# Starting the aggregation products on Y's upper half before the last five adjacency rows are prepared, and moving part of the column sums to TensorE

## The chip, the cores and the metric

The kernel runs on one core of a Trainium2 chip. The metric is the device time of one execution in microseconds (us); lower is better. A core has TensorE (PE, matrix products and transposes), VectorE (DVE), ScalarE (ACT), GpSimd (POOL) and SyncE (SP), which here issues nearly all DMAs. The engines run their own instruction lists in order and wait for each other on semaphores.

## The reference: what is computed

Inputs are x (8 batches, 2048 nodes, 128 features) and adj (2048 x 2048), all in float32. Cut to what matters:

```python
HW = einsum('bnf,fo->bno', layernorm(x), W)
A  = relu((adj + adj.T) * 0.5)
D  = sum(A, axis=1)
d  = where(D > 0, D ** -0.5, 0)
L  = eye(N) - d[:, None] * A * d[None, :]
x  = x + relu(einsum('nm,bmo->bno', L, HW))
x  = x + moe(layernorm(x))      # tokens + 8 gated experts, top 2, GELU between two 128x128 products
```

The change touches only the part before and around the first rows of the einsum with L.

## The kernel before, in words

**Layout.** The nodes are cut into 16 blocks of 128. S = relu(adj + adj.T) is symmetric, so only its lower triangle of 136 blocks of 128 x 128 is kept (`s_tri`). The features of half of the batches (4) lie side by side as 512 columns: Y, in 16 node blocks, is HW scaled by d. Each float32 operand of the large products is split in a high and a low part (`y0_hi`, `y0_lo`, `stage[..][hi, lo]`), and a block of a product is three 128 x 512 matmuls.

**Stage one, the setup loop.** The rows of S are made from j = 15 down to 0; r = 15 - j counts them. For one row SP loads the row of adj (`low`) and its column (`up`) into one of nine slots; PE transposes the column's blocks into PSUM (`turn`, in groups of four, 40 groups in all), DVE adds the row (`add`), ACT applies relu in place and sums along the row (`relu`). POOL and, for j = 5 to 1, DVE add each row to running column sums (`add_columns`). A node's degree is its row sum plus its column sum; the sum over partitions of column block k is a product with a column of ones (`column_sum(k)`). Between the rows, a job k (0 to 15) brings one node block of x: SP loads it (`load`), DVE takes mean and variance (`statistics`), POOL inverts (`invert`), PE transposes it (`turn_x`) and multiplies by W (`project`), ACT copies (`copy_x`) and keeps the result in `hw0` (`keep`). `JOBS` says how many jobs go ahead of each row: 2 for rows r = 0 to 3, then 1 each for r = 4 to 11.

**Degrees.** `degrees(0)` on DVE finishes blocks 8 to 15, POOL takes the power -1/2 (`root(0)`), ACT makes the high part of Y (`y_high(m)`) and DVE the low part (`y_low(m)`); `degrees(1)` and `root(1)` do blocks 7 to 0.

**Stage two, the products.** Unit u of the einsum is node block 15 - u. Its matrix operand is staged: blocks that lie in the triangle as they are (`high_direct`, `low_direct`), the others transposed by PE in groups of four (`turn_group(u, g)`), copied by ACT (`high_group`) and finished by DVE (`low_group`). Units 0 and 1 are made in four parts of eight blocks each: unit 0 with Y's blocks 15 to 8, unit 1 with the same, unit 0 with blocks 7 to 0, unit 1 with those. From unit 2 on a unit is one run of sixteen blocks, and while it runs the next one's operand is staged. After the 32 units (16 for each half of the batches) come the expert layers.

**Order.** All of it is written out by hand: each engine's function lists its steps, with tables such as `JOBS`, `RELU_AT`, `ADD_AT` and `PARTS_AT` for what stands between the `y_high`/`y_low` steps.

## Time and profile before

| | |
|---|---|
| median of 3 runs | 878.15 us (875.48 to 878.35) |
| the profiled execution | 877.46 us, of which the traced span is 875.7 us |
| TensorE busy | 839.2 us, 96% of the span |
| VectorE, ScalarE, GpSimd busy | 639.1, 476.0 and 324.7 us |
| first product of unit 0, first product of unit 2 | 78.62 us and 108.07 us from the span's start |

Times below are from the start of the span. Names such as L692 are lines of the kernel. In the trace a float32 matmul that isn't a transpose is listed as two matmuls (a 128 x 1 column sum counts x2), a transpose as one. Matmuls are pipelined: a listed duration reaches past the start of the next one, so spacing is read from the start times.

### The profile page before, as it was taken

To read this page: it belongs to the slowest core of one execution; us is meant where nothing else is said; L and a number is where in the kernel's file an instruction comes from. 1 tells how busy PE (TensorE), PEld (TensorE's weight loads), DVE (VectorE), ACT (ScalarE), POOL (GpSimd) and SP (SyncE) were. 2 spreads that over 40 slices of the span, in tenths; PEclk is the share of its full clock that TensorE was granted. 3 is DMA by queue.
4 is the path that set the end of the run, shared out by engine and by line. 5 is a ranking of instruction groups with operands and counts; after the bars stand their busy time and mean duration, and the time that the engine had idled before them with its cause. 6 is when DMAs were issued, how large, how long until landed. Compare 5 with 4: busy or idle time off the path is not lost.

```text
span 875.7 us, 14324 instructions
## 1 busy us (share of the span) xinstructions
PE 839.2 (96%) x4098; PEld 697.3 (80%) x4098; DVE 639.1 (73%) x1553; ACT 476.0 (54%) x871; POOL 324.7 (37%) x318
## 2 busy tenths in 40 slices
PE   3687999999999999999999999999999999999998
PEld 3676788888888888888888777788888888888886
DVE  3678645479889644443515599999999999999997
ACT  2686523224333201021110488888888888888886
POOL 1893163474757545555445539101000000000000
PEclk9999999999999999999999999999999999999999
DMA  9991576686866257977778876778767777778772
GB/s 277 325 311 53 220 284 253 240 277 237 272 221 202 85 181 285 334 273 263 255 280 315 303 249 230 267 281 294 289 272 265 257 274 277 273 290 292 286 266 82
DMA packets 93472, 223.00 MB, mean 255 GB/s; under 512 B 8904, under 2 KB 60128, under 8 KB 81520
## 3 DMA queue, kind: packets, MB, share of 16 engines
q1 hardware_dynamic: 88304, 213.23, 68.7%
q0 software_dynamic: 2608, 8.33, 2.4%
q10 hardware_dynamic: 2512, 0.86, 0.4%
q8 instruction: 24, 0.39, 0.2%
q14 instruction: 24, 0.20, 0.1%
HBM read 157.89 MB, written 64.49 MB: 254 GB/s over the span
## 4 chain that ended last, share of the span: by engine, by line
PE 90%; DVE 4%; ACT 2%; DMA 2%; issue 1%; DVEq 0%; ACTq 0%; SPq 0%
PE bank L989 13%; PE bank L991 13%; PE bank L990 13%; PE bank L1489 6%; PE bank L1473 6%; PE bank L1475 6%; PE bank L1486 6%; PE bank L1474 6%; PE bank L1487 6%; PE bank L344 3%; PE bank L936 2%; PE bank L1495 2%; PE bank L474 1%; PE bank L325 1%; DMA b_sb<-in_L_ffn_b 1%
## 5 line engine op out<-in xcount | busy, mean ns | idle before, releaser
L1531 ACT ACTIVATE act_h<-bank,b_sb 128x512 f32<-128x512 f32 x256 | 176.3, 689 | 46.8 <-PE bank L1475 42.5
L1573 DVE TENSOR_TENSOR gated<-c_all,act_h 128x512 f32<-128x512 f32 x256 | 177.4, 693 | 25.5 <-ACT act_h L1531 20.4
L1578 DVE TENSOR_TENSOR g_lo<-gated,g_hi 128x512 fp32r<-128x512 f32 x256 | 175.1, 684 | 0.2
L1538 ACT ACTIVATE g_hi<-gated 128x512 fp32r<-128x512 f32 x256 | 159.5, 623 | 6.1 <-DVE gated L1573 6.1
L1449 POOL DMA_DIRECT2D out<-fin x31 | 23.6, 762 | 308.6 <-DVE fin L1586 308.6
L1105 POOL TENSOR_SCALAR z<-x,mv,rstd 128x128 f32<-128x128 f32 x128 | 106.9, 848 | 3.4
L989 PE MATMUL bank<-y_hi,stage 128*128 128x512 f32 x256 | 105.4, 412 | 2.8 <-issue 1.6
L1051 ACT ACTIVATE z_hl<-bank 128x512 fp32r<-128x512 f32 x32 | 19.1, 597 | 156.4 <-PE bank L936 156.4
L1473 PE MATMUL bank<-z_e,w_hi 128*128 128x512 f32 x256 | 102.8, 402 | 0.1
L1489 PE MATMUL bank<-g_lo,w_hi 128*128 128x512 f32 x256 | 100.9, 394 | 1.1 <-DVE g_lo L1578 1.1
L989 PE MATMUL bank<-y,stage 128*128 128x512 f32 x256 | 101.2, 395 | 0.0
L1486 PE MATMUL bank<-g_hi,w_lo 128*128 128x512 f32 x256 | 100.1, 391 | 0.5 <-ACT g_hi L1538 0.5
L991 PE MATMUL bank<-y_hi,stage 128*128 128x512 f32 x256 | 100.4, 392 | 0.0
L1475 PE MATMUL bank<-z_e,w_lo 128*128 128x512 f32 x256 | 99.9, 390 | 0.0
L990 PE MATMUL bank<-y_lo,stage 128*128 128x512 f32 x256 | 99.9, 390 | 0.0
L991 PE MATMUL bank<-y,stage 128*128 128x512 f32 x256 | 99.9, 390 | 0.0
L1474 PE MATMUL bank<-z_e,w_hi 128*128 128x512 f32 x256 | 99.8, 390 | 0.0
L990 PE MATMUL bank<-y,stage 128*128 128x512 f32 x256 | 99.7, 389 | 0.0
L1487 PE MATMUL bank<-g_hi,w_hi 128*128 128x512 f32 x256 | 99.7, 389 | 0.0
L1100 POOL TENSOR_TENSOR rstd<-var_eps,neg_half 128x4 f32<-128x4 f32 x32 | 37.2, 1162 | 148.5 <-DVE var_eps L1155 148.5
L1159 DVE TENSOR_TENSOR z_hl<-bank,z_hl 128x512 fp32r<-128x512 f32 x32 | 22.0, 687 | 78.4 <-ACT z_hl L1051 78.4
L1489 PEld LDWEIGHTS bank<-g_lo,w_hi 128*128 128x128 f32 x256 | 48.0, 188 | 14.6 <-DVE g_lo L1578 4.7
(133 smaller groups left out, 1487.4 us busy)
## 6 DMA issues: line engine op xcount, KB each, us to landing
c_all<-c_scratch SPq DMA_DIRECT2D x64, 1024.0 KB, 8.1
s_scratch<-stage SPq DMA_DIRECT2D x14, 2048.0 KB, 8.2
stage<-s_scratch SPq DMA_DIRECT2D x14, 2048.0 KB, 8.0
z_e<-z_scratch SPq DMA_DIRECT2D x32, 512.0 KB, 7.3
z_scratch<-z_hl SPq DMA_DIRECT2D x31, 512.0 KB, 2.7
x_raw<-in_x SPq DMA_DIRECT2D x32, 256.0 KB, 6.7
x_res<-in_x SPq DMA_DIRECT2D x32, 256.0 KB, 7.0
r_e<-res_scratch SPq DMA_DIRECT2D x32, 256.0 KB, 2.7
```

What stands on the lines that cost most here:

```text
L989: pe.matmul(out[:, :], s_hi, y_hi, start=(i == 0), stop=False)
L990: pe.matmul(out[:, :], s_hi, y_lo, start=False, stop=False)
L991: last = pe.matmul(out[:, :], s_lo, y_hi, start=False, stop=(i == MB - 1))
L1473: pe.matmul(ps_h[k][:, :], v.w1_hi[:, e, :], v.z_e[s][:, 0, :], start=True, stop=False)
L1474: pe.matmul(ps_h[k][:, :], v.w1_hi[:, e, :], v.z_e[s][:, 1, :], start=False, stop=False)
L1475: pe.matmul(ps_h[k][:, :], v.w1_lo[:, e, :], v.z_e[s][:, 0, :], start=False, stop=True).then_inc(h_done, 1)
L1486: pe.matmul(ps_o[s][:, :], v.w2_lo[:, e, :], hi[:, :], start=False, stop=False)
L1489: pe.matmul(ps_o[s][:, :], v.w2_hi[:, e, :], lo[:, :], start=False, stop=(e == E - 1)).then_inc(o_done, 1)
L1531: act.activation(v.act_h[e % R][:, :], ps_h[e % 2][:, :], ACT.Gelu, bias=v.b1_sb[:, e:e + 1]).then_inc(gelu_done, 1)
L1538: act.activation(v.g_hi[e % R][:, :], v.gated[e % R][:, :], ACT.Copy).then_inc(hi_done, 1)
L1573: dve.tensor_tensor(out=v.gated[e % R][:, :], in0=v.c_all[s][:, e, :], in1=v.act_h[e % R][:, :], op=ALU.mult).then_inc(gated_done, 1)
L1578: dve.tensor_tensor(out=v.g_lo[e % R][:, :], in0=v.gated[e % R][:, :], in1=v.g_hi[e % R][:, :].bitcast(FP32), op=ALU.subtract).then_inc(lo ...
```

## The change: what it does

- The loop over rows stops after r = 10 (j = 5). `degrees(0)` and the diagonal blocks of units 0 and 1 come in that last row. Rows j = 4 and 3 are transposed just before the first product, rows j = 2, 1, 0 by `turn_last` behind unit 0's blocks 14, 13 and 12. ACT applies relu to all five of them after the eight `y_high` steps of the upper half.
- `JOBS` now has fourteen jobs in the loop. The x blocks of jobs 14 and 15 get two buffers of their own (`x_raw` 4 and 5), are loaded after the rows and are transposed and projected between products of parts 1 and 2.
- The first two transposed groups of unit 0 (`(0, 0)`, `(0, 1)`) are made in rows r = 8 and r = 10.
- `LAST` goes from 6 to 9: POOL adds rows 14 to 9 to the column sums, DVE adds 8, 7 and 6 later, in one place. Rows 5 to 1 are added nowhere: `column_sum(k)` for k = 4 to 0 takes one product with ones for each of them in the same PSUM column, 5 + 4 + 3 + 2 + 1 = 15 more products. The sums k = 15 to 12 follow row r = 6, 11 to 8 follow r = 10, and 7 to 0 stand in part 1 of the products.
- PSUM banks and load slots are given by tables (`BANK`, `SLOT`).

```diff
-    LAST = 6
+    LAST = 9
+    ADDED = 6
+    ROWS_APART = 11
-    JOBS = [2, 2, 2, 2, 1, 1, 1, 1, 1, 1, 1, 1, 0, 0, 0, 0]
+    JOBS = [2, 2, 2, 2, 1, 1, 1, 1, 1, 1, 0, 0, 0, 0, 0, 0]
+    EARLY = sum(JOBS)
...
# column_sum on PE
-                wait(pe, col_added, min(14 - k, 14))
-            pe.matmul(ps_d[part_of(k)][:, k:k + 1], column, v.one_col[:, :], start=True, stop=True).then_inc(col_done, 1)
+                wait(pe, col_added, min(14 - k, 15 - ADDED))
+            rest = range(k + 1, ADDED)
+            if rest:
+                pe.wait_ge(relued, until_row(k + 1))
+            last = pe.matmul(ps_d[part_of(k)][:, k:k + 1], column, v.one_col[:, :], start=True, stop=not rest)
+            for j in rest:
+                last = pe.matmul(ps_d[part_of(k)][:, k:k + 1], s_tri[:, block(j, k), :], v.one_col[:, :], start=False,
+                                 stop=(j == ADDED - 1))
+            last.then_inc(col_done, 1)
...
# ACT after the loop over eleven rows
+            if r == 10:
+                pr.keep(act, EARLY - 1)
+            if r in (8, 10):
+                st.high_group(act, 0, r // 2 - 4)
         st.high_direct(act, 0)
+        for m in range(15, 7, -1):
             y_high(m)
+        st.high_direct(act, 1)
+        st.high_group(act, 1, 0)
+        st.high_group(act, 1, 1)
+        for r in range(ROWS_APART, MB):
+            for g in range(n_groups(MB - 1 - r)):
+                relu(r, MB - 1 - r, g)
+        pr.copy_x(act, 14)
...
# PE, the last rows of the loop
+            if r == 6:
+                for k in (15, 14, 13, 12):
+                    column_sum(k)
+            if r == 8:
+                pe.wait_ge(relued, until_row(MB - 1))
+                st.turn_group(pe, 0, 0)
+            if r == 10:
+                for k in (11, 10, 9, 8):
+                    column_sum(k)
+                pr.project(pe, EARLY - 1)
+                st.turn_group(pe, 0, 1)
+        turn(11, 4, 0)
+        turn(11, 4, 1)
+        turn(12, 3, 0)
...
# DVE, the end of the loop and what follows
+            if r == 10:
                 degrees(0)
                 for u in range(2):
                     st.diagonal(dve, u)
+                st.low_group(dve, 0, 1)
+        add(11, 4, 0)
+        add(11, 4, 1)
         st.low_direct(dve, 0)
+        add(12, 3, 0)
+        y_low(15)
+        y_low(14)
+        add(13, 2, 0)
+        y_low(13)
+        add(14, 1, 0)
+        y_low(12)
+        add(15, 0, 0)
+        for m in range(11, 7, -1):
             y_low(m)
+        st.low_direct(dve, 1)
+        st.low_group(dve, 1, 0)
+        st.low_group(dve, 1, 1)
+        for j in (8, 7, 6):
+            add_columns(j)
+        degrees(1)
+        pr.statistics(dve, 14)
+        st.low_group(dve, 0, 2)
+        y_low(7)
+        y_low(6)
+        pr.statistics(dve, 15)
...
# PE, parts 0 to 2 of the products
-            if part == 0:
-                for k in range(4, -1, -1):
-                    v.column_sum(k)
+                if part == 0 and m in row_at:
+                    v.turn_last(row_at[m], MB - 1 - row_at[m], 0)
+                if part == 1 and m == 14:
+                    pr.turn_x(pe, 14)
+                if part == 1 and m == 11:
+                    pr.project(pe, 14)
+                if part == 1 and m == 10:
+                    for k in range(7, -1, -1):
+                        v.column_sum(k)
+                if part == 1 and m == 9:
+                    pr.turn_x(pe, 15)
+                if part == 2 and m == 6:
+                    pr.project(pe, 15)
```

Three places where the order of instructions moves. The first is PE's list from the last column sum of the loop to the second block of unit 0, in the kernel before (L692 is `turn`, L344 `project`, L474 `turn_group`, L989 to L991 one block of products):

```order
L703 MATMUL bank<-one_col,col_sum 128x1
L692 MATMUL bank<-ident,up_101 128x128 x2
L692 MATMUL bank<-ident,low_100 128x128
L344 MATMUL bank<-gnn_w_sb,x_t_115 128x128 x4
L692 MATMUL bank<-ident,up_103 128x128
L692 MATMUL bank<-ident,low_102 128x128 x2
L474 MATMUL bank<-ident,s_tri 128x128 x7
L989 MATMUL bank<-y_hi,stage_96 128x512
L990 MATMUL bank<-y_lo,stage_96 128x512
L991 MATMUL bank<-y_hi,stage_96 128x512
```

The same engine in the changed kernel, from the second block of products (m = 14) to the fourth (L733 is `turn`, L1059 to L1061 a block of products):

```order
L1059 MATMUL bank<-y_hi,stage_96 128x512
L1060 MATMUL bank<-y_lo,stage_96 128x512
L1061 MATMUL bank<-y_hi,stage_96 128x512
L733 MATMUL bank<-ident,up_101 128x128 x2
L733 MATMUL bank<-ident,low_100 128x128
L1059 MATMUL bank<-y_hi,stage_96 128x512
L1060 MATMUL bank<-y_lo,stage_96 128x512
L1061 MATMUL bank<-y_hi,stage_96 128x512
L733 MATMUL bank<-ident,up_103 128x128
L733 MATMUL bank<-ident,low_102 128x128
```

Before, all rows were transposed ahead of the first product; now the last three stand one by one between blocks.

The second place is DVE at the same point of the program. Before (L734 is `add`, L464 `low_direct`, L488 `low_group`, L767 `y_low`, L743 `add_columns`):

```order
L734 TENSOR_TENSOR s_tri<-bank,low_102 128x128
L464 TENSOR_TENSOR stage_96<-s_tri,stage_96 128x128
L488 TENSOR_TENSOR stage_96<-bank,stage_96 128x384
L767 SCALAR_TENSOR_TENSOR y_lo<-hw_95,d_inv,y_hi 128x512 x2
L488 TENSOR_TENSOR stage_96<-bank,stage_96 128x512
L767 SCALAR_TENSOR_TENSOR y_lo<-hw_95,d_inv,y_hi 128x512
L743 TENSOR_TENSOR col_sum<-col_sum,s_tri 128x512
```

And in the changed kernel (L509 is `low_group`, L788 `add`, L483 `low_direct`, L821 `y_low`):

```order
L509 TENSOR_TENSOR stage_96<-bank,stage_96 128x512
L788 TENSOR_TENSOR s_tri<-bank,low_98 128x4x128
L788 TENSOR_TENSOR s_tri<-bank,low_98 128x128
L483 TENSOR_TENSOR stage_96<-s_tri,stage_96 128x128
L788 TENSOR_TENSOR s_tri<-bank,low_100 128x4x128
L821 SCALAR_TENSOR_TENSOR y_lo<-hw_95,d_inv,y_hi 128x512 x2
L788 TENSOR_TENSOR s_tri<-bank,low_100 128x3x128
L821 SCALAR_TENSOR_TENSOR y_lo<-hw_95,d_inv,y_hi 128x512
L788 TENSOR_TENSOR s_tri<-bank,low_102 128x2x128
L821 SCALAR_TENSOR_TENSOR y_lo<-hw_95,d_inv,y_hi 128x512
```

The additions of the last rows, which stood ahead of all `y_low`, now stand between them, and `low_group` of (0, 1) stands ahead of them all.

The third place is PE in part 1, where the column sums now stand together (L747 is the first product of a `column_sum`, L749 the added ones):

```order
L747 MATMUL bank<-one_col,col_sum 128x1 x4
L749 MATMUL bank<-one_col,s_tri 128x1
L747 MATMUL bank<-one_col,col_sum 128x1
L749 MATMUL bank<-one_col,s_tri 128x1 x2
L747 MATMUL bank<-one_col,col_sum 128x1
L749 MATMUL bank<-one_col,s_tri 128x1 x3
L747 MATMUL bank<-one_col,col_sum 128x1
L749 MATMUL bank<-one_col,s_tri 128x1 x4
L747 MATMUL bank<-one_col,col_sum 128x1
L749 MATMUL bank<-one_col,s_tri 128x1 x5
```

These are 23 products of one column; between parts 0 and 1 the kernel before had five.

## Rows read from the trace of the kernel before

**Rows 1.** The page: busy time of PE, and the chain that ended last.

```profile
PE 839.2 (96%) x4098; PEld 697.3 (80%) x4098; DVE 639.1 (73%) x1553; ACT 476.0 (54%) x871; POOL 324.7 (37%) x318
PE 90%; DVE 4%; ACT 2%; DMA 2%; issue 1%; DVEq 0%; ACTq 0%; SPq 0%
```

**Rows 2.** Waits of PE, 57 to 110 us: total us, times, longest.

```profile
PE bank L692 <- DVE s_tri L734: 2.8, 2, 2.0
PE bank L692 <- issue: 2.5, 3, 1.3
PE bank L989 <- issue: 1.6, 1, 1.6
PE bank L989 <- DVE y_lo L767: 1.2, 3, 0.7
```

**Rows 3.** Timeline of PE: start, us, instruction, [idle before and its end].

```profile
59.23 0.95 PE L692 MATMUL bank<-ident,up 128*128 128x128 f32 x7 [1.29 <-issue]
...
62.61 0.84 PE L692 MATMUL bank<-ident,up 128*128 128x128 f32 x6 [0.82 <-issue]
...
65.54 0.74 PE L692 MATMUL bank<-ident,up 128*128 128x128 f32 x5 [0.41 <-issue]
...
78.62 0.47 PE L989 MATMUL bank<-y_hi,stage 128*128 128x512 f32 x1 [1.56 <-issue]
...
80.50 0.50 PE L989 MATMUL bank<-y_hi,stage 128*128 128x512 f32 x1 [0.26 <-DVE y_lo L767]
...
108.07 0.39 PE L989 MATMUL bank<-y_hi,stage 128*128 128x512 f32 x1
```

**Rows 4.** The chain of waits: start, us it holds the chain, what.

```profile
60.41 0.49 PE bank L325 x4
60.90 0.89 PE bank L344 x8
...
86.15 0.24 PE bank L991
86.39 1.01 PE bank L703 x10
...
88.88 0.44 PE bank L474 x4
```

**Rows 5.** Windows: busy us of each engine, then granted PE clock, DMA share, GB/s.

```profile
74.00:75.00 1.00, 0.90 (x5) 0.60 (x3) 1.00 (x3) 0.23 (x2) 1.00 (x2) 0.50 0.00 0
```

**Rows 6.** Timeline of SP: issue of job 14's load.

```profile
55.78 2.23 SPq L272 DMA_DIRECT2D x_raw<-in_x  x1
```

**Rows 7.** Timeline of DVE.

```profile
63.27 1.16 DVE L734 TENSOR_TENSOR s_tri<-bank,low 128x512 f32<-128x512 f32 x2 [2.10 <-PE bank L692]
...
73.47 0.83 DVE L743 TENSOR_TENSOR col_sum<-col_sum,s_tri 128x640 f32<-128x640 f32 x1
...
79.70 0.74 DVE L767 SCALAR_TENSOR_TENSOR y_lo<-hw,d_inv,y_hi 128x512 fp32r<-128x512 f32 x1
...
87.50 0.17 DVE L752 TENSOR_TENSOR deg_raw<-bank,deg_row 128x8 f32<-128x8 f32 x1 [1.37 <-PE bank L703]
...
90.58 0.75 DVE L767 SCALAR_TENSOR_TENSOR y_lo<-hw,d_inv,y_hi 128x512 fp32r<-128x512 f32 x1 [1.71 <-ACT y_hi L644]
```

**Rows 8.** Line L449, the diagonal steps, 60 to 75 us: duration in ns min/median/max, starts.

```profile
L449 DVE SCALAR_TENSOR_TENSOR s_tri<-ident,deg_neg,s_tri x2: 351/1126/1901, 66.8 to 67.1; 128x128 f32<-128x128 f32 x2
```

**Rows 9.** Timeline of ACT.

```profile
61.85 1.11 ACT L356 ACTIVATE hw<-bank,x_rstd 128x128 f32<-128x128 f32 x4
...
77.02 1.32 ACT L644 ACTIVATE y_hi<-hw,d_inv 128x512 fp32r<-128x512 f32 x2
...
89.83 0.72 ACT L644 ACTIVATE y_hi<-hw,d_inv 128x512 fp32r<-128x512 f32 x1 [5.07 <-POOL d_inv L610]
```

**Rows 10.** Timeline of POOL.

```profile
66.93 1.89 POOL L604 TENSOR_TENSOR col_sum<-col_sum,s_tri 128x768 f32<-128x768 f32 x1
...
72.40 1.64 POOL L610 TENSOR_TENSOR d_inv<-deg_safe,neg_half 128x8 f32<-128x8 f32 x1
```

More of the change, by code:

```diff
@@ L236, in project_program @@
     Q, CW, MB = v.Q, v.CW, v.MB
-    ps_x, ps_p = v.banks[4], [v.banks[5] if k % 2 or k >= v.MB else v.banks[3] for k in range(v.U)]
+    BANK = [3 if k in range(0, 14, 2) else 6 if k == 14 else 5 for k in range(v.U)]
+    ps_x, ps_p = v.banks[4], [v.banks[b] for b in BANK]
     pr = Plan()
-    x_in = [sem(f"x_in{i}") for i in range(4)]
+    x_in = [sem(f"x_in{i}") for i in range(6)]
     w_mean_done = sem("w_mean_done")
@@ L259, in place, with last_before @@
         return (0, MB - 1 - k) if k < MB else (1, k - MB)
+    SLOT = [k % 4 if k < 14 else (5, 4)[k - 14] if k < MB else k % 2 for k in range(v.U)]
     def slot(k):
-        return k % 4 if k < MB else k % 2
+        return SLOT[k]
     def loads_until(k):
-        return 16 * (k // 4 + 1) if k < MB else 16 * (MB // 4 + (k - MB) // 2 + 1)
+        return 16 * SLOT[:k + 1].count(SLOT[k])
+    def last_before(names, k):
+        return max([i + 1 for i in range(k) if names[i] == names[k]] + [0])
     def load(sp, k):
         h, m = place(k)
-        free = k - 3 if k < MB else k - 1
+        if k in (14, 15):
+            sp.wait_ge(v.summed, v.until_tenth)
+        free = last_before(SLOT, k)
         wait(sp, xt_turned, free)
@@ L582, in sync @@
                              v.adj[0:j * P, j * P:(j + 1) * P].rearrange("(i p) n -> p i n", p=P)).then_inc(up_in[s], 16)
+        for k in range(EARLY, MB):
+            pr.load(sp, k)
     def gpsimd(pool):
@@ L622, in gpsimd @@
                 add_columns(j)
-            if r == 10:
+            if r == 9:
                 root(0)
         root(1)
+        for k in range(EARLY, MB):
+            pr.invert(pool, [k])
     def scalar(act):
@@ L657, in scalar @@
                     pr.keep(act, k - 1)
-        act.wait_ge(pr.xt_turned, MB)
-        act.wait_ge(pr.x_mv_done, MB)
+            if r == 10:
+                pr.keep(act, EARLY - 1)
+            if r in (8, 10):
+                st.high_group(act, 0, r // 2 - 4)
         st.high_direct(act, 0)
-        st.high_group(act, 0, 0)
-        for m in range(MB - 1, -1, -1):
+        for m in range(15, 7, -1):
             y_high(m)
-            if m in RELU_AT:
-                relu(MB - 1 - RELU_AT[m], RELU_AT[m], 0)
-            if m == 7:
-                pr.keep(act, MB - 1)
-            for u, g in PARTS_AT.get(m, ()):
-                if g is None:
-                    st.high_direct(act, u)
-                else:
-                    st.high_group(act, u, g)
+        st.high_direct(act, 1)
[5 more added lines that the diff above has]
+        pr.copy_x(act, 14)
+        act.wait_ge(pr.xt_turned, EARLY)
+        act.wait_ge(pr.x_mv_done, EARLY)
+        st.high_group(act, 0, 2)
+        y_high(7)
+        y_high(6)
+        pr.copy_x(act, 15)
+        y_high(5)
+        st.high_group(act, 0, 3)
+        pr.keep(act, 14)
+        y_high(4)
+        y_high(3)
+        st.high_group(act, 1, 2)
+        pr.keep(act, 15)
+        y_high(2)
+        y_high(1)
+        st.high_group(act, 1, 3)
+        y_high(0)
     def tensor(pe):
@@ L713, in tensor @@
                 turn(r, j, g)
-            if j + 2 < MB and r < 13:
-                column_sum(j + 2)
-            if r == 13:
-                pr.project(pe, MB - 1)
-        pe.wait_ge(deg_step, 2)
-        pe.wait_ge(pr.hw_kept, MB - 1)
-        for g in range(2):
-            st.turn_group(pe, 0, g)
-        v.column_sum = column_sum
+            if r == 6:
[12 more added lines that the diff above has]
+        turn(12, 3, 0)
+        v.column_sum, v.turn_last = column_sum, turn
     def vector(dve):
@@ L771, in vector @@
         pr.centre_w(dve)
[L772 to L775 removed]
+        for r, j in enumerate(ROWS[:ROWS_APART]):
+            for k in jobs(r):
+                pr.statistics(dve, k)
             for g in range(n_groups(j)):
                 add(r, j, g)
[L778 to L780 removed]
             if r == 9:
+                st.low_group(dve, 0, 0)
+            if r == 10:
                 degrees(0)
@@ L784, in vector @@
                     st.diagonal(dve, u)
-            if r == 11:
-                add_columns(5)
+                st.low_group(dve, 0, 1)
+        add(11, 4, 0)
+        add(11, 4, 1)
         st.low_direct(dve, 0)
-        st.low_group(dve, 0, 0)
-        for m in range(MB - 1, -1, -1):
-            y_low(m)
-            if m in ADD_AT:
-                add_columns(ADD_AT[m])
-            for u, g in PARTS_AT.get(m, ()):
-                if g is None:
-                    st.low_direct(dve, u)
-                else:
-                    st.low_group(dve, u, g)
-                if (u, g) == (1, 0):
-                    degrees(1)
-            if m == 3:
-                outward()
+        add(12, 3, 0)
[7 more added lines that the diff above has]
+        for m in range(11, 7, -1):
+            y_low(m)
+        st.low_direct(dve, 1)
[9 more added lines that the diff above has]
+        pr.statistics(dve, 15)
+        y_low(5)
+        st.low_group(dve, 0, 3)
+        y_low(4)
+        y_low(3)
+        st.low_group(dve, 1, 2)
+        y_low(2)
+        y_low(1)
+        st.low_group(dve, 1, 3)
+        outward()
+        y_low(0)
     stage = Plan()
```

52 lines of the change are left out of this document (24 added, 28 removed).

## The prediction, written before the changed kernel was run

> **What bounds the kernel now.** I read the page first: PE is busy 96% of the span and holds 90% of the chain that ended last [rows 1]. From unit 2 on PE runs without gaps, so whatever the change does is decided by when unit 2 begins, 108.07 us before [rows 3]; the rest should follow by the same amount. Second, PE's waits up to there: 2.8 us for `add`, 2.5 us for the landing of rows ("issue"), 1.6 us ahead of the first product, 1.2 us for `y_low`, with the small one for x about 8.5 us [rows 2]. Third, the windows: between two of these gaps PE's granted clock is 0.50 of full, 1.2 instead of 2.4 GHz [rows 5], after an idle stretch of 2.0 us [rows 2]. So the stage holds some 8.5 us of waits, and a little for the clock, that a better order could win. Last, the engines' timelines, for durations.
>
> **Two ways to count.** The new unit 2 starts at (first product) + (PE work between it and unit 2) + (PE waits between them). I work out each.
>
> **The first product.** The two x loads that are taken out stood ahead of rows r = 10 and 11 (issue at 55.78 [rows 6]). Each is 256 KB, 0.8 us of a queue that moves some 320 GB/s, so r = 10 can be transposed at 65.54 - 0.8 = 64.7 instead of 65.54 [rows 3]; rows r = 8 and 9 keep their 59.23 and 62.61 [rows 3]. Transposing r = 10 takes until 65.6. The four column sums 11 to 8 behind it take 4 x 0.2 = 0.8 (five take 1.01, [rows 4]), so they end at 66.4, `project(13)` (0.89, [rows 4]) at 67.3, `turn_group` (0, 1) (0.44) at 67.75, `turn` of r = 11 at about 68.3. PE then waits: the transpose of r = 12 needs `add(11, 0)`, and that stands on DVE behind `low_group(0, 1)`, which needs ACT's `high_group(0, 1)`, which stands behind `keep(13)`. ACT: `keep(13)` starts when the projection is out, 67.4, and takes 1.0 (1.11 [rows 9] with its overlap); the group's copy, about 0.5, ends at 68.95. DVE: `low_group` until 69.6, `add(11, 0)` until 70.3 (two additions of 512 and 384 columns take 1.16 [rows 7], one of 512 about 0.68). PE transposes r = 12 from 70.35 and has it out at 70.95. `add(12)` takes 0.6, `y_low(15)` starts at 71.6, and a product starts 0.80 after its `y_low` starts (79.70 [rows 7], 80.50 [rows 3]): 72.4. The degrees don't hold it: `degrees(0)` ends about 67.2, `root(0)` (1.64 [rows 10]) 68.9, ACT's `y_high(15)` at 69.2. So the first product starts 6.2 us earlier than its 78.62 [rows 3]. In this stretch POOL's three largest remaining column additions are gone, and one of them (1.89 at 66.93 [rows 10]) lay over the second diagonal step, which took 1.90 where the first took 0.35 [rows 8]; my chain has the pair at 0.6. I count nothing for DVE's own additions of rows 8, 7, 6: 0.83 for 640 columns [rows 7], so about 3.5 for 1024, 896 and 768, hidden under part 1; with that cover gone they would cost the 3.5.
>
> **PE work up to unit 2.** Before, from 78.62 to 108.07 [rows 3] are 29.45 us, of which 1.2 are waits [rows 2]: 28.2. Added to it: rows 13 to 15, six small transposes, 0.9 (four take 0.44 [rows 4]); two x blocks, 2 x (0.49 + 0.89) = 2.7 [rows 4]; 23 column sum products instead of 5. Five take 1.01 [rows 4], so 18 more take 3.7. Sum 35.5. Of this, 15 x 0.2 = 3.1 us is work that PE did not have at all before; the rest is only moved. Hence, without any wait after the first product, unit 2 would start at 72.4 + 35.5 = 107.9, which is where it started before. That is the core of the forecast: 6.2 us of head start are spent on moved and new work, and each wait comes on top.
>
> **PE waits after the first product.** (a) Rows 13, 14, 15 stand alternately on both engines. After block 14 PE transposes row r = 13 (out about 74.4); only then can DVE add it (0.5) and make `y_low(13)`, whose product may start 0.80 after: 75.7, while PE was free at 74.25. Wait 1.45. The same for r = 14 (0.35 for the addition): 1.35; for r = 15 (0.2): 1.2. Sum 4.0; DVE idles in the same places, since `y_low(11)` to `y_low(8)`, which need no row, stand behind them. Upper half done at 83.9. What else is queued behind: ACT's `high_direct(1)` needs all rows summed, about 79.4, and the five relus stand behind it, until about 86; nobody needs these before PE's column sums near 90. (b) Part 1 runs from 83.9. The column sums stand after its sixth block, start near 89.9 and end at 94.7. From the last column sum to the `y_low` it feeds: DVE takes it up at 87.50, ACT's `y_high` starts at 89.83, `y_low` at 90.58 [rows 7, 9], 3.1 us, then 0.80 to the product. So block 7 of unit 0 can start at 94.9 + 3.1 + 0.8 = 98.8. PE's cover is two blocks (0.69 each), one group and one x transpose: 2.3, free at 97.05. Wait 1.7. (c) Part 2: DVE has `statistics(15)` (1.45) between `y_low(6)` and `y_low(5)`: wait 0.35. ACT has `keep(14)` and `keep(15)` (1.0 each) and its groups between the `y_high` steps, of 0.61 each (1.32 for two [rows 9], less overlap); by this row `y_high(2)` starts at 104.45 and its product at 105.95, PE free at 104.65: wait 1.3; last block: 0.55. Sum of (a) to (c): 4.0 + 1.7 + 2.2 = 7.9.
>
> **Sum.** 72.4 + 35.5 + 7.9 = 115.8 against 108.07: +7.7. On the profiled execution's own time, 877.46 + 7.7 = 885.2; it lies 0.7 below the median of the three runs, so that a median is likely to show 885 to 886. I take 885. Nothing is added for the clock: before, it fell after 2.0 us of idling [rows 2, 5]; the new stretch has 2.0 us, then 1.4, then the three of (a), so it may fall again, and every block at 1.2 GHz costs 0.7 more.
>
> **A rule weighed.** POOL's additions are the only long POOL work that the trace shows over DVE: 66.93 to 68.82 [rows 10], and the second diagonal step, begun at 67.1, ends some 0.2 behind it [rows 8]. The small ones don't do it: the 0.83 column addition [rows 7] began within POOL's 1.64 [rows 10] and is in line with the 0.68 of an addition of 512. The Trainium skill, page "SBUF — State Buffer", section "Who interferes with whom", has it that a DVE step with two SBUF inputs and a GpSimd step exclude each other for the whole instruction, whatever its size. By that rule the diagonal pair would wait for `root(0)` (until 68.9, +0.4 on the first product), and `y_low(5)` for the inversion of job 15 (+1.0); the sum would be 1.4 more, 886.6. By the row the sum stays. I go by the row.
> A second rule: the page "TensorE: Matmul & The Clock Gate" (section "Wait — 56ns, not 53.3ns?") gives about 25 ns as the least distance of two matmuls, and by that the 15 new products (30 passes) would be an estimated 0.75 us instead of 3.1 and the time 882.8. The row measures 0.10 a pass for just this instruction [rows 4], and decides.
>
> **The rivals.**
> 1. Slower by about 7 us as summed, 4 to 10: 0.66.
> 2. The waits mostly vanish. If the ping-pong of (a) is shorter than I count or ACT's order in (c) is harmless, what stays is (b) and the moved work: 72.4 + 35.5 + 1.7 = 109.6, +1.5, 879; with every wait gone 877.3. For it: my waits hang on chains of four short steps each; against it: each link has a row. 0.15, half of it within 0.3%.
> 3. The clock falls in the stretch from 72 to 80. Four to six blocks at half speed, 0.7 each, less what the waits hide: +2 to +4, 887 to 889. For it: [rows 5]; against: a wait of 1.6 us before the first product did not do it. 0.12.
> 4. Faster than before. It needs the first product before 69.8 and no wait behind it, since 69.8 + 35.5 = 105.3. The place is `add(11, 0)`: were ACT's group (0, 1) out when DVE reaches it, `y_low(15)` would be bound by `y_high(15)`, 69.2, its 0.6 and the product's 0.8: 70.6, +35.5 = 106.1 and, without waits, 875.5; at 70.6 with only (b) it is 877.2. It decides only below 69.8, which needs the rows or the upper degrees some 1 us earlier as well. 0.07.
>
> **How the numbers follow.** About 0.3%, 2.6 us, is what a measurement of this kernel can tell from no change. Faster by more: rival 4, 0.07. Within: most of rival 2 and the low edge of my case, 0.12. Slower: the rest, 0.81. The range takes in rival 2's middle and rival 3: 878 to 889.5; below lies about 0.1, above 0.06. The likeliest case's own range is 881 to 888.
>
> **What would show it.** First product near 72.4 (right if 71.5 to 73.5); PE idle three times for `y_low` by 1.2 to 1.5 between it and the fifth block; the 23 column sums holding 4.6 to 5; a wait of 1.5 to 2 ahead of part 2's first block, and one over 1 before its sixth block; unit 2 near 115.8. POOL has no step over 2.5 us after 60 us, and the diagonal pair takes about 0.6. The forecast is wrong if unit 2 starts before 110, which would need the waits of (a) gone or the column sums at a quarter of their row.

## The result, and the profile after

| | before | after |
|---|---|---|
| median | 878.40 us (875.48 to 880.07, 6 runs) | 893.41 us (891.09 to 894.76, 6 runs) |
| ratio, with its 95% interval | | 1.0171 [1.015, 1.0192] |
| the profiled execution | 877.46 us | 892.67 us, span 891.0 us |
| first product of unit 0 | 78.62 us | 73.01 us |
| first product of unit 2 | 108.07 us | 121.83 us |

The changed kernel is slower by 15.0 us of median. The forecast was 885.0 us, +6.9, with a range of 878 to 889.5: the sign is right, the size is less than half of what was measured, and the time lies above the range. Single runs far above the rest (969.37 us in spread_sums, 1217.65 and 2181.13 us among the runs of the kernel before) are in no median of an experiment, range or ratio below. From the page of the profile after, the engines' busy time, TensorE's granted clock over 40 slices, and the chain that ended last (the first and third line stand against [rows 1]):

```profile
PE 848.6 (95%) x4128; PEld 704.8 (79%) x4128; DVE 638.7 (72%) x1551; ACT 476.1 (53%) x871; POOL 319.2 (36%) x315
PEclk9997899999999999999999999999999999999999
PE 85%; ACT 4%; DMA 3%; DVE 3%; POOL 3%; issue 1%; DVEq 0%; ACTq 0%; SPq 0%
```

PE has 30 more instructions, the 15 added column-sum products, and is busy 9.4 us longer. Thirty products of one column are no 9.4 us at the 0.1 us a pass of [rows 4]: something that stays busy has become slower. The second line says where to look, at slices 4 and 5 (67 to 111 us), where the mean granted clock is 0.7 and 0.8. Nearly all of the loss is there: unit 2 starts 13.76 us later, and the profiled execution ends 15.21 us later. The remaining 1.5 us isn't shown to come from the change: the time from unit 2's start to the end was between 769.0 and 771.0 us in the profiled executions of all the kernels below (769.4 before, 770.8 after).

PE's waits from 0 to 140 us in the profile after, to be read against [rows 2] (the rest of the list lies ahead of 57 us):

```profile
PE bank L1059 <- DVE y_lo L821: 5.2, 6, 1.3
PE bank L733 <- issue: 3.0, 3, 1.4
PE bank L733 <- DVE s_tri L788: 2.2, 1, 2.2
PE bank L1059 <- DVE s_tri L788: 1.5, 1, 1.5
```

Six waits for `y_low`, 5.2 us together, stand behind the first product. PE's timeline shows where they are; it stands against [rows 3]:

```profile
70.89 0.52 PE L733 MATMUL bank<-ident,up 128*128 128x128 f32 x3 [2.15 <-DVE s_tri L788]
...
73.01 0.47 PE L1059 MATMUL bank<-y_hi,stage 128*128 128x512 f32 x1 [1.49 <-DVE s_tri L788]
...
77.49 0.50 PE L1059 MATMUL bank<-y_hi,stage 128*128 128x512 f32 x1 [1.31 <-DVE y_lo L821]
...
79.85 0.50 PE L1059 MATMUL bank<-y_hi,stage 128*128 128x512 f32 x1 [1.18 <-DVE y_lo L821]
...
82.43 0.80 PE L1059 MATMUL bank<-y_hi,stage 128*128 128x512 f32 x1 [1.04 <-DVE y_lo L821]
...
94.03 0.95 PE L747 MATMUL bank<-one_col,col_sum 128*128 128x1 f32 x8
...
98.56 2.27 PE L749 MATMUL bank<-one_col,s_tri 128*128 128x1 f32 x10
100.70 0.77 PE L1059 MATMUL bank<-y_hi,stage 128*128 128x512 f32 x1
...
112.09 0.50 PE L1059 MATMUL bank<-y_hi,stage 128*128 128x512 f32 x1 [1.16 <-DVE y_lo L821]
...
121.83 0.39 PE L1059 MATMUL bank<-y_hi,stage 128*128 128x512 f32 x1
```

Two things are to be read here. The three waits of the alternation (rows transposed between blocks, and added between `y_low` steps) are 1.31, 1.18 and 1.04. And the column sums, 46 passes (a pass is one of the two matmuls of a float32 product), hold PE from 94.03 to 100.70, 6.7 us; the first eight take 0.10 each (94.03 to 94.83, from the timeline at that place), the last ten 0.21 (98.56 to 100.70). The windows of the profile after (length, busy time of PE, PEld, DVE, ACT and POOL, granted clock, DMA share, GB/s) show why; they stand against [rows 5]:

```profile
73.30:76.50 3.20, 2.88 (x9) 1.88 (x7) 0.55 (x2) 1.20 (x2) 0.00 (x0) 0.52 0.00 0
80.40:87.00 6.60, 5.56 (x17) 3.96 (x17) 3.70 (x7) 1.12 (x3) 0.00 (x0) 0.50 0.01 2
97.30:104.10 6.80, 6.80 (x30) 6.40 (x30) 2.67 (x15) 0.84 (x2) 2.51 (x2) 0.50 0.00 0
...
88.00:97.00 9.00, 9.00 (x64) 8.11 (x62) 3.28 (x4) 3.19 (x12) 0.00 (x0) 1.00 0.00 1
96.00:97.00 1.00, 1.00 (x11) 1.00 (x11) 0.00 (x0) 0.00 (x0) 0.00 (x0) 1.00 0.00 0
98.00:99.00 1.00, 1.00 (x7) 1.00 (x6) 0.00 (x0) 0.00 (x0) 0.00 (x0) 0.50 0.00 0
```

Three stretches have the clock at half, 1.2 instead of 2.4 GHz, 16.6 us in all; the kernel before had one from about 73 to 76.5 us, and from 80 to 105 us none. PE works 2.88 + 5.56 + 6.80 = 15.24 us in them, at half speed, so about 7.6 us are lost. The first two stretches follow waits of PE. The third doesn't: PE is busy all the time from 88 to 97 and at 98, and the clock falls in the middle of the products of one column.

That closes the account from the first product to unit 2, 121.83 - 73.01 = 48.8 us: 35.5 of work as forecast, 5.2 of waits, 7.6 for the clock, and 0.5 that stays over.

The engine behind those waits, in DVE's timeline (against [rows 7, 8]):

```profile
67.75 0.61 DVE L468 SCALAR_TENSOR_TENSOR s_tri<-ident,deg_neg,s_tri 128x128 f32<-128x128 f32 x2
...
76.22 0.56 DVE L788 TENSOR_TENSOR s_tri<-bank,low 128x384 f32<-128x384 f32 x1 [2.65 <-PE bank L733]
...
87.92 3.47 DVE L797 TENSOR_TENSOR col_sum<-col_sum,s_tri 128x1024 f32<-128x1024 f32 x3
...
100.94 0.17 DVE L806 TENSOR_TENSOR deg_raw<-bank,deg_row 128x8 f32<-128x8 f32 x1 [9.45 <-PE bank L749]
```

DVE waits for PE (2.65 at 76.22) just before PE waits for DVE (1.31 at 77.49). The three additions of rows 8, 7 and 6 take 3.47 and are hidden; DVE then idles 9.45 us for the last column sum.

### The profile page after: what moved, and what is told of

Read it like the earlier page. It is cut to its first block, busy times and chain, and to the rows that moved or that the text cites. A ratio compares the mean times of both kernels' runs of the same rounds, so it can differ in the third digit from the quotient of the medians.

```text
span 891.0 us, 14375 instructions
## 1 busy us (share of the span) xinstructions
PE 848.6 (95%) x4128; PEld 704.8 (79%) x4128; DVE 638.7 (72%) x1551; ACT 476.1 (53%) x871; POOL 319.2 (36%) x315
## 4 chain that ended last, share of the span: by engine, by line
PE 85%; ACT 4%; DMA 3%; DVE 3%; POOL 3%; issue 1%; DVEq 0%; ACTq 0%; SPq 0%
PE bank L1059 13%; PE bank L1061 13%; PE bank L1060 13%; PE bank L1570 6%; PE bank L1554 6%; PE bank L1556 6%; PE bank L1567 6%; PE bank L1555 6%; PE bank L1568 6%; PE bank L355 3%; POOL expo L1201 3%; PE bank L1006 2%; ACT s_tri L663 1%; PE bank L338 1%; PE bank L495 1%
## 5 line engine op out<-in xcount | busy, mean ns | idle before, releaser
L1059 PE MATMUL bank<-y_hi,stage 128*128 128x512 f32 x256 | 107.5, 420 | 6.7 <-DVE y_lo L821 5.2
L1061 PE MATMUL bank<-y_hi,stage 128*128 128x512 f32 x256 | 101.8, 398 | 0.0
L1059 PE MATMUL bank<-y,stage 128*128 128x512 f32 x256 | 101.2, 395 | 0.0
L1061 PE MATMUL bank<-y,stage 128*128 128x512 f32 x256 | 99.9, 390 | 0.0
L1059 PEld LDWEIGHTS bank<-y_hi,stage 128*128 128x128 f32 x256 | 49.0, 191 | 17.8 <-DVE y_lo L821 7.3
```

The lines of the kernel that those rows point to most:

```text
L1059: pe.matmul(out[:, :], s_hi, y_hi, start=(i == 0), stop=False)
L1061: last = pe.matmul(out[:, :], s_lo, y_hi, start=False, stop=(i == MB - 1))
```

## The experiments

The theory after the result: the work and the waits are about as forecast, and what is missing is half clock, twice behind waits of PE and once in the run of products of one column. The rival: PE's work was underpriced (above all the 15 added products, or the moved steps), and the clock only accompanies it.

Each ratio is against runs of the kernel before taken alongside, whose medians lie between 878.07 and 878.87; "less than the changed kernel" is against its 893.41. The profiled executions can't be compared by their end alone. Row r = 10 stands ahead of every edit in the changed kernel and the seven variants of it, and still its transposes begin anywhere from 62.87 to 67.98, with the landing of the rows:

```profile
65.12 0.74 PE L733 MATMUL bank<-ident,up 128*128 128x128 f32 x5 [1.12 <-issue]
```

This is the row in the changed kernel; its start is the first column below, in us from the span's start. What an edit did is read between two of the three points:

| profiled execution | row r = 10 | first product | unit 2 |
|---|---|---|---|
| before | 65.54 | 78.62 | 108.07 |
| after | 65.12 | 73.01 | 121.83 |
| fill_waits | 65.14 | 73.02 | 117.79 |
| rows_ahead | 67.66 | 77.67 | 119.39 |
| no_ones | 63.39 | 71.92 | 115.97 |
| before_plus_ones | 66.12 | 78.94 | 112.71 |
| wide_instead | 65.62 | 74.25 | 121.52 |
| spread_sums | 62.87 | 70.75 | 120.14 |
| rows_ahead_no_ones | 65.49 | 74.76 | 112.17 |
| all_mended_filled | 67.98 | 77.93 | 112.97 |
| before_diag_later | 66.41 | 77.68 | 107.38 |
| before_diag_later_filled | 64.59 | 75.87 | 105.34 |

### Filling the waits: fill_waits

`fill(pe, 8, 12, 384)` is 8 products of 384 columns into an unused bank.

```diff
+        fill(pe, 8, 12, 384)
         turn(12, 3, 0)
+        fill(pe, 6, 12, 384)
...
                     v.turn_last(row_at[m], MB - 1 - row_at[m], 0)
+                    v.fill(pe, 5, 12, 384)
```

> The changed kernel with extra 384-column products into a bank that is free there, whose results nobody reads: 8 and 6 in PE's two waits ahead of the first product of unit 0, 5 behind each of the three rows that stand between its blocks. They fit into the waits, so the order and the waits for DVE stay. Theory 1 (half of the loss beyond the sum is the clock, 0.50 from 73.3 to 76 us and from 80.3 to 87 us in the changed kernel's trace, and the idling ahead of it brings the fall): the clock stays at 1.0 in 73 to 90 us, unit 2 begins 3 to 4.5 us earlier than its 121.8, the time is 889 to 890.5. Rival (the waits alone make the loss, the clock would have fallen anyway): the clock falls at the same places, the time stays at 893 or rises by up to 1.

Measured: 889.80 us (888.49 to 890.85, 4 runs), ratio 1.0137 [1.0092, 1.0181], 3.6 us below the changed kernel although PE has 29 more products to make. The windows of its profile:

```profile
66.00:92.00 26.00, 23.90 (x144) 20.19 (x145) 15.79 (x32) 13.57 (x38) 1.64 (x1) 1.00 0.15 43
...
94.00:100.00 6.00, 6.00 (x25) 5.60 (x26) 2.64 (x15) 0.81 (x2) 2.48 (x2) 0.50 0.00 0
```

The first product starts at 73.02, as after, and the clock is 1.00 from 66 to 92, so the first two stretches are gone; unit 2 starts at 117.79, 4.04 earlier, where half of PE's 8.44 us in those stretches is 4.2. The chip does more work in less time, which a price of the work can't explain. The third stretch is there as before, at 94 to 100: it isn't a consequence of the first two.

### Only the rows ahead: rows_ahead

```diff
         turn(12, 3, 0)
+        turn(13, 2, 0)
+        turn(14, 1, 0)
+        turn(15, 0, 0)
...
         add(12, 3, 0)
-        y_low(15)
-        y_low(14)
         add(13, 2, 0)
-        y_low(13)
         add(14, 1, 0)
-        y_low(12)
         add(15, 0, 0)
-        for m in range(11, 7, -1):
+        for m in range(15, 7, -1):
             y_low(m)
...
-        row_at = {14: 13, 13: 14, 12: 15}
+        row_at = {}
```

> The changed kernel with rows 13 to 15 transposed and added ahead of the first y_low instead of between the blocks. Theory 1: the first product moves from 73.0 to about 74.2, the three waits of 1.3, 1.2 and 1.0 us between the blocks go, and with them the second stretch at half clock (2.8 us); the first one may stay, since the idling ahead of it does. Sum -1.2 + 3.5 + 2.8 = 5 us less: 887.5 to 889.5. Rival (the alternation is hidden, since DVE's y_low steps are the limit): 892 to 894.

Measured: 886.60 us (884.99 to 889.10, 5 runs), ratio 1.0095 [1.006, 1.0129]: 6.8 us less than the changed kernel, and 0.9 below the expected range, which had summed 5. In the profiles, from row r = 10 to unit 2 it is 51.7 instead of 56.7, so 5.0 less. The alternation cost waits of 3.5, and the second stretch of half clock; taking it out gives both back, less a first product that starts later. The profiled execution was the slowest of the five, 889.10, and still has a half clock behind the waits ahead of its first product:

```profile
77.00:83.00 6.00, 5.33 (x13) 4.25 (x14) 5.54 (x9) 1.09 (x3) 0.00 (x0) 0.50 0.01 3
```

Its own first product starts at 77.67, 4.7 later than in the changed kernel: 2.5 of it is the later landing of row r = 10, 1.2 was expected from the edit, and the rest fits the clock, which was at half just ahead of it too (0.78 on average from 66 to 72). Where the clock falls isn't fixed by the list of instructions: the changed kernel has it whole from 66 to 68, no_ones, whose list on every engine is the same up to there, has it at half. So one profile alone doesn't give the price of an edit.

```profile
66.00:68.00 2.00, 2.00 (x12) 2.00 (x11) 0.62 (x2) 1.30 (x5) 1.50 (x1) 0.50 0.95 261
```

### Only the added products out: no_ones

```diff
-    ADDED = 6
+    ADDED = 1
...
-        for j in (8, 7, 6):
+        for j in (8, 7, 6, 5, 4, 3, 2, 1):
```

> The changed kernel with ADDED = 1: rows 5 to 1 are added to the column sums by DVE, behind rows 8, 7 and 6, and each column sum is one product again, 8 in part 1 instead of 23. Theory 1: 15 products less are 3.3 us at full clock, and the third stretch at half clock (97.3 to 104.1 us, 3.3 us lost), which begins while PE runs only one-column products, goes or shrinks; against it part 2 now has to wait for the degrees by about 1.7, since its cover runs at full speed. 887.5 to 889.5. DVE's five further additions (2.8 us) lie in its 9.5 us wait. Rival (the clock falls there whatever stands in part 1): only the 3.3 us go, 889.5 to 890.5. A second rival (DVE's additions come too late): PE waits for col_added and the time is 892 or more.

Measured: 888.97 us (886.09 to 891.30, 4 runs), ratio 1.0133 [1.0086, 1.0181], 4.4 us less. The runs spread over both expectations, so the time doesn't decide between them; the clock does. In the profiled execution (886.09, the fastest) unit 2 starts at 115.97, 5.9 earlier, of which 1.7 is the earlier landing of row r = 10. The 30 passes are gone and the clock at their place is whole, but a wait comes back: from the first product to unit 2 it is 44.1 instead of 48.8. The window and the first product of part 2 in this kernel:

```profile
97.00:105.00 8.00, 6.14 (x33) 4.56 (x31) 6.86 (x20) 7.00 (x17) 3.45 (x5) 1.00 0.24 98
```

```profile
99.02 0.47 PE L1059 MATMUL bank<-y_hi,stage 128*128 128x512 f32 x1 [1.67 <-DVE y_lo L821]
```

The prediction had a wait of 1.7 at this place. In the changed kernel it is 0, since PE at half clock comes too late to wait.

### The added products alone, in the kernel before: before_plus_ones

```diff
-    ADD_AT = {13: 4, 11: 3, 10: 2, 9: 1}
+    ADD_AT = {}
...
-                wait(pe, col_added, min(14 - k, 14))
-            pe.matmul(ps_d[...], column, v.one_col[:, :], start=True, stop=True).then_inc(col_done, 1)
+                wait(pe, col_added, min(14 - k, 9))
+            rest = range(k + 1, 6) if k < 5 else range(0)
+            if rest:
+                pe.wait_ge(relued, until_row(k + 1))
+            last = pe.matmul(ps_d[...], column, v.one_col[:, :], start=True, stop=not rest)
+            for j in rest:
+                last = pe.matmul(ps_d[...], s_tri[:, block(j, k), :], v.one_col[:, :], start=False,
+                                 stop=(j == 5))
+            last.then_inc(col_done, 1)
...
-            if r == 11:
-                add_columns(5)
```

> The kernel before with this one part of the change: DVE adds none of rows 5 to 1, and the column sums 4 to 0 between parts 0 and 1 take the 15 further products with ones. Theory 1: +3.1 us of PE work less at most 1 us for the relief of DVE, and if the run of 20 one-column products brings the clock down, up to 2 more: 880.5 to 883.5. Rival (DVE's five additions, 2.8 us, were on the path of y_low, so that the part pays for itself): 877 to 879.

Measured: 883.06 us (881.39 to 885.39, 10 runs), ratio 1.0058 [1.0039, 1.0077]. This is the cleanest case, since PE waits for nothing from 81 to 104 us. Two rows of PE's timeline, the last run of one-column products and the second wide one behind it, and then the windows:

```profile
89.21 1.25 PE L708 MATMUL bank<-one_col,s_tri 128*128 128x1 f32 x10
...
90.72 0.63 PE L995 MATMUL bank<-y_lo,stage 128*128 128x512 f32 x1
```

```profile
88.00:90.00 2.00, 2.00 (x21) 2.00 (x20) 0.00 (x0) 0.00 (x0) 0.00 (x0) 1.00 0.00 0
90.00:92.00 2.00, 2.00 (x10) 1.59 (x10) 1.27 (x5) 0.00 (x0) 0.77 (x1) 0.64 0.04 8
92.00:94.00 2.00, 2.00 (x8) 1.70 (x7) 0.35 (x1) 1.10 (x3) 1.49 (x3) 0.51 0.00 0
```

PE is busy all the time, the 40 passes from 85.94 to 90.33 take 0.11 each, and just behind them the clock is at half until about 94. The 30 added passes are thus worth 4.4 - 1.0 = 3.4 directly, and the clock about 1.7 more (3.4 us at half speed). From the first product to unit 2 it is 33.8 instead of 29.5, so 4.3 longer: the two together are 5.1, one wait for `y_low` of 0.3 is gone, and 0.5 stays unexplained. Of unit 2's start at 112.71, 4.6 later than before, 0.3 stands ahead of the first product.

The clock fell inside or just behind this run in all four kernels that have it unbroken: the changed kernel, fill_waits, rows_ahead (at half from 97) and before_plus_ones.

### The same total time in wide products: wide_instead

no_ones, with 19 extra products of 384 columns where the column sums begin. Their target bank holds job 14's projection, so the x block of that job is not the reference's.

```diff
                 if part == 1 and m == 10:
+                    v.fill(pe, 19, 12, 384)
                     for k in range(7, -1, -1):
```

> The kernel of no_ones with 19 extra products of 384 columns ahead of its 8 column sums in part 1, 0.17 us each, 3.3 us in all: as much PE time at full clock as the 15 products with ones that they stand for; nobody reads their results. Theory (it is the run of one-column products that brings the clock down in part 1, not the PE time in front of it): the granted clock stays at 1.0 from the end of the second stretch on, until a wait of PE; the column sums end 3.3 us later than in no_ones, and the time is 891.5 to 893. Rival (any 5 us run between the waits does it, the second stretch of idling coming late): half clock at the same place as in the changed kernel.

Measured: 889.90 us (888.53 to 891.61, 4 runs), ratio 1.0132 [1.0099, 1.0165]. The row of the extra products, and the windows over and behind them:

```profile
95.35 3.48 PE L739 MATMUL bank<-stage 128*128 128x384 f32 x19
```

```profile
95.00:99.00 4.00, 4.00 (x26) 3.92 (x24) 1.18 (x4) 0.00 (x0) 0.00 (x0) 1.00 0.00 0
99.00:119.00 20.00, 16.64 (x90) 13.16 (x90) 13.47 (x41) 11.33 (x25) 4.71 (x5) 1.00 0.54 208
```

With as much PE time in wide products the clock stays at 1.00, so it is the run of one-column products, and not how long PE works without a pause, that brings it down. The loads of the stationary operand alone don't do it either: PEld is busy for 3.92 of these 4.00 us. The time missed the expected 891.5 to 893: its median is only 0.9 above no_ones. In the profiles the step from the first product to unit 2 is 47.3 against 44.1, 3.2 more where 3.3 were expected; medians of four runs that spread over 3.1 and 5.2 us don't show it.

### Spreading the column sums: spread_sums

```diff
-                if part == 1 and m == 10:
-                    for k in range(7, -1, -1):
-                        v.column_sum(k)
+                for k in {12: (7, 6, 5, 4), 11: (3, 2), 10: (1,), 9: (0,)}.get(m, ()) if part == 1 else ():
+                    v.column_sum(k)
```

> The changed kernel with the 23 one-column products spread over part 1: sums 7 to 4 behind its block 12, 3 and 2 behind 11, 1 behind 10 and 0 behind 9; nothing is left out. Theory 1 (the unbroken run of one-column products brings the clock down, though PE is never idle in it): the third stretch at half clock is gone, 3.3 us; but the degrees' chain of 3.9 us after the last sum now has a cover of 1.6 at full clock, so a wait of 2 to 2.5 us ahead of part 2 comes back: 891 to 893. Rival (the clock falls in part 1 because of the waits before it or of something else): still half clock near 97 to 104 us, 893 or more.

Measured: 893.7 us (889.11 to 894.46, 4 runs), ratio 1.0184 [1.0165, 1.0203]: no gain, and 0.7 above the expected range. The profiled execution is the fastest, 889.11, and the one in which row r = 10 came earliest; from that row to unit 2 it is 57.3, against 56.7 in the changed kernel. It shows what went where, first in PE's timeline and then in the windows:

```profile
102.24 0.76 PE L1059 MATMUL bank<-y_hi,stage 128*128 128x512 f32 x1 [2.85 <-DVE y_lo L821]
```

```profile
86.00:101.00 15.00, 13.39 (x95) 11.88 (x93) 5.75 (x18) 3.54 (x13) 2.04 (x2) 1.00 0.00 1
102.00:105.00 3.00, 2.76 (x7) 2.21 (x8) 2.89 (x13) 3.00 (x8) 0.68 (x1) 0.50 0.02 5
```

Between blocks of products the one-column ones no longer bring the clock down, but the last of them ends one block nearer to part 2, the wait ahead of it grows to 2.85, where 2 to 2.5 were expected, and the clock falls behind that wait.

### Both out, and both out with the waits filled: rows_ahead_no_ones, all_mended_filled

The first is the edits of rows_ahead and no_ones together. The second adds 8 products of 384 columns ahead of row r = 12 and 4 ahead of the first product.

> Both earlier edits in the changed kernel: rows 13 to 15 ahead of the first y_low, and one product for each column sum with DVE adding rows 5 to 1. Singly they took 6.8 and 4.4 us off the 893.4. Theory 1 (waits, clock and added work are separate costs): together 882 to 884; what is left against the kernel before are the wait ahead of part 2 (about 1.7 us) and those of part 2 (about 2), and the moved x blocks. Rival (they mend the same loss, the clock): 885 to 887.

Measured: 883.68 us (881.56 to 885.15, 4 runs), ratio 1.0072 [1.0054, 1.009], 9.7 us below the changed kernel. Unit 2 starts at 112.17 in its profile; the clock is at half once, from about 73.1 to 79.9, around the wait ahead of the first product:

```profile
74.00:79.00 5.00, 4.24 (x10) 3.40 (x11) 5.00 (x9) 1.17 (x3) 0.00 (x0) 0.50 0.01 3
```

> The kernel of rows_ahead_no_ones with extra 384-column products in PE's waits, eight ahead of row 12 and four ahead of the first product, results unread. Theory (three separate costs: waits, clock, added work; with the last two taken out only waits and moved work are left): clock 1.0 from 66 to 95 us, about 1.5 to 2 below the 883.7: 881.5 to 882.5, still 3 to 4 above the kernel before, from the wait ahead of part 2 (1.7) and those within it. Rival (without the clock the change has no loss left): 878 to 879.5.

Measured: 880.00 us (877.99 to 882.24, 10 runs), ratio 1.0019 [1.0006, 1.0032], between the two expectations. The profiled execution, the slowest of the ten, has the clock at half from 70 to 73 and whole from 74 to 100. From row r = 10 to unit 2 it is 45.0 there, against 42.5 in the kernel before. So with the alternation, the added products and nearly all of the half clock taken out, what is left of the change costs 0.2%, with the 12 added products that fill the waits: starting on the upper half has by itself no gain here. What is left of waits is 3.3 us for `y_low`, 1.65 of it ahead of part 2.

### The kernel before, its own gap: before_diag_later, before_diag_later_filled

In the kernel before, POOL's addition lies over the second diagonal step [rows 8, 10]. The first moves the diagonal steps one row later; the second also fills two waits of PE.

```diff
             if r == 9:
                 degrees(0)
+            if r == 10:
                 for u in range(2):
                     st.diagonal(dve, u)
...
+            if r == 12:
+                fill(pe, 2, 256)
...
         for g in range(2):
             st.turn_group(pe, 0, g)
+        fill(pe, 2, 256)
```

> The kernel before with the two diagonal steps of DVE moved from row r = 9 to behind the additions and statistics of row r = 10. Theory (the 1.9 us of the second diagonal step is a wait for POOL's addition of 768 columns that ran at the time, not work): the pair takes 0.6 at its new place, add(11) and with it PE's wait of 2.0 us ahead of row 12 come 1.5 us earlier, and the clock may no longer fall behind it (another 1.4): 875.5 to 877.2. Rival (the wait moves to the next DVE step with two inputs in SBUF, or the rows' landing binds instead): 878 to 879.

Measured: 876.88 us (876.33 to 878.43, 11 runs), ratio 0.9984 [0.9971, 0.9997]. DVE's timeline in this kernel:

```profile
69.73 0.38 DVE L289 BATCH_NORM_AGGREGATE x_mv<-x_stats 128x2 f32<-128x6 f32 x4 [0.44 <-issue]
...
70.23 0.60 DVE L449 SCALAR_TENSOR_TENSOR s_tri<-ident,deg_neg,s_tri 128x128 f32<-128x128 f32 x2
```

The pair takes 0.60, where the two steps took 0.35 and 1.90 before [rows 8]. The statistics step now stands under POOL's addition, which ends at 69.58, and idles 0.44 before its next part; the profile doesn't say for what. Unit 2 starts at 107.38, 0.7 earlier, but the rows landed 0.9 later in this execution: from row r = 10 to unit 2 it is 41.0 instead of 42.5, about the 1.5 us of the stall. The clock still falls, now behind the wait ahead of the first product:

```profile
78.00:81.40 3.40, 3.40 (x10) 2.63 (x9) 3.40 (x7) 3.40 (x10) 0.00 (x0) 0.50 0.00 0
```

> The kernel of before_diag_later with four extra products of 256 columns in PE's two waits, two ahead of row 12 and two ahead of the first product of unit 0; their results go to a part of a bank that nobody reads. Theory (the idling ahead of 73 us brings the clock down): granted clock 1.0 from 66 to 90 us, 875 to 876.5, at most 1.4 below before_diag_later. Rival (the clock does not fall there any more once the wait is short, and the extra products only stand in the way): 0.5 to 1 above before_diag_later.

Measured: 875.91 us (874.97 to 879.17, 11 runs), ratio 0.9987 [0.9976, 0.9998], against a median of 878.07 for the kernel before in the same runs. The window of its profile:

```profile
62.00:100.00 38.00, 33.56 (x194) 27.01 (x193) 29.54 (x84) 26.51 (x68) 12.18 (x10) 1.00 0.38 127
```

The clock is whole from 62 to 100, and unit 2 starts at 105.34, 2.7 earlier than before; but 0.95 of that is the earlier landing of row r = 10, and from there to unit 2 it is 40.8, against 41.0 without the filling. So here a whole clock won almost nothing: where PE worked at half speed in before_diag_later, it waits in part for `y_low` now (0.24 and 0.29 ahead of the third and fourth block). This is the fastest version by median. Both intervals stay below 1, but the gain of 0.1 to 0.2% is less than what one such measurement can tell from no change, and the second is not told apart from the first.

## Why the prediction was right or wrong

**The first product: right.** Forecast 72.4, measured 73.01. The chain is the one that was worked out (`high_group`, `low_group`, `add(11, 0)`, transpose, `add(12)`, `y_low(15)`), and runs about 0.5 late because the rows landed later: r = 8 at 59.78 instead of 59.23, r = 10 at 65.12 instead of 64.7.

**The work up to unit 2: right.** 35.5 forecast, 36.0 measured once waits and clock are taken out. The added products cost 0.10 to 0.11 a pass at full clock, as [rows 4] had it. One term was added up wrongly: six small transposes at the row's 0.44 for four are 0.66, not 0.9, so the forecast's own rows give 35.3. The rule weighed against the row, of the Trainium skill, page "TensorE: Matmul & The Clock Gate", section "Wait — 56ns, not 53.3ns?", gives a least distance of about 25 ns. That is a floor and not the price of this instruction: the trace after shows 0.10 at full clock and 0.21 at half.

**The waits: right in place, somewhat too large.** (a) 4.0 forecast, 1.31 + 1.18 + 1.04 = 3.5 measured. (b) 1.7 forecast, 0 measured in the changed kernel, because PE was slow, and 1.67 in no_ones, where it wasn't. (c) 2.2 forecast, 0.19 + 1.16 + 0.35 = 1.7 measured. Sum 5.2 instead of 7.9. Of the signs that the prediction named, the first product and the wait over 1 before part 2's sixth block came, and the three waits of (a) but for the size of the last; the wait ahead of part 2's first block, the time of the column sums (6.7 for 4.6 to 5) and unit 2's start did not.

**"Nothing is added for the clock": the step that failed.** The prediction named the condition, a wait of 2.0 us followed by more of them, and priced the clock at nothing in the sum; rival 3 had it as one stretch, +2 to +4, with a chance of 0.12. Measured are three stretches and 7.6 us, less the 1.7 that they hide of wait (b). The first two are rival 3, in two stretches instead of one, 4.2 us: fill_waits gets 3.6 us of median back by work that keeps PE busy in the gaps. The argument against it, that a wait of 1.6 ahead of the first product did not do it before, took one wait by itself where the change makes five within fourteen us. The third was in no case of the prediction: 23 column sums were priced as work at full clock, 4.7, and the run of them brings the clock down with PE never idle, as before_plus_ones and wide_instead show from both sides. The run took 6.7; at the 0.11 a pass of before_plus_ones it would be 5.1, so 1.6 of the difference is the clock, and the blocks and groups behind the run up to 104 lose about as much again.

**The sum, put right.** 73.0 + 36.0 + 5.2 + 7.6 = 121.8, where the forecast had 72.4 + 35.5 + 7.9 = 115.8. The 6.0 between them is +0.6, +0.5, -2.7 and +7.6. The difference between the profiled executions behind unit 2, 1.5, was not forecast either, and lies in the spread that all the kernels have there.

**The rule on the shared port: the row was right to decide for DVE.** The diagonal pair took 0.61 from 67.75 while POOL's power ran from 67.59 for 1.64 us:

```profile
67.59 1.64 POOL L634 TENSOR_TENSOR d_inv<-deg_safe,neg_half 128x8 f32<-128x8 f32 x1 [3.35 <-DVE deg_safe L810]
```

So POOL's powers on a few columns don't hold up DVE here, where the Trainium skill, page "SBUF — State Buffer", section "Who interferes with whom", has the later one block when a DVE step with two inputs in SBUF meets a GpSimd step that reads SBUF; POOL's wide addition did hold DVE up, in [rows 8, 10]. The other way round the trace agrees with the page: the inversion of job 15 began just behind DVE's `y_low(5)` and took 1.45 instead of the 1.01 that it takes by itself (at 103.22).

```profile
106.78 0.74 DVE L821 SCALAR_TENSOR_TENSOR y_lo<-hw,d_inv,y_hi 128x512 fp32r<-128x512 f32 x1
```

```profile
106.94 1.45 POOL L311 TENSOR_TENSOR x_rstd<-x_var,neg_half 128x4 f32<-128x4 f32 x1 [2.71 <-DVE x_var L306]
```

**What stays open.** Why executions with the same list differ in where the clock falls and in when the rows land; what it is in a run of one-column products that brings the clock down; and whether the gain of before_diag_later_filled over before_diag_later is real.

## What to carry to other kernels

A wait on TensorE can be paid twice when others stand near it: once as idle time, once as half clock on the work behind it. Price both, and fill a gap that can't be closed; it pays where the work behind it has no other wait to take up what the clock gives back. Where single profiles are compared, first find a point ahead of the edit, and count from there: here it moved by up to 5.1 us between executions with the same list up to it. Work is moved to TensorE as products of one column at the price of its time and of the clock behind it; a long run of them is busy in the profile's count and still brings the clock down, so it is split by wide products, and not just ahead of a point where something waits for the last of them. And when a head start is bought by placing two engines' steps alternately, first add up the work without any wait: here it came out at 107.9 against 108.07, so that there was nothing to win, and every wait was a loss.

## What the runs showed of the hardware

- The granted clock fell from 1.00 (96 to 97) to 0.50 (98 to 99) inside an unbroken run of one-column float32 products with PE busy 1.00, and behind such a run in before_plus_ones; 19 products of 384 columns at the same place left it at 1.00.
- At half clock a one-column pass took 0.21 us instead of 0.10 to 0.11, so its price goes with the clock and isn't a fixed time.
- POOL's powers on 128 x 8 (1.64 us) left two DVE steps with two inputs in SBUF at their usual time (0.61 for the pair), POOL's addition of 768 columns (1.89 us) stretched one from 0.35 to 1.90, and a POOL power on 128 x 4 that began behind such a DVE step took 1.45 us instead of 1.01.
- Filling PE's waits with products that nobody reads kept the clock at 1.00 from 66 to 92 us and made the kernel 3.6 us faster, with 29 more products.
